# A perceiver layer with routed experts: the entries' product moved into an up product, and a sorted copy of the rows

## The chip, the cores and the metric

The kernel runs on one core of one Trainium2 chip. The metric is the device time of one execution in microseconds (us). Before the change three runs gave 350.67, 354.34 and 351.03 us, median 351.03.

## The reference

One layer over 512 tokens (4 batches of 128 rows, 512 features) and a context of 4 x 2048 rows of 384 features: cross attention, causal self attention, then a feed forward part with one shared expert and 16 routed ones, of which each token takes 4. Each part has its layer norm and its residual. Only the last part is touched:

```python
def _L0_ffn_ref(hidden_states, gate_w, bias_e, up_w, down_w, shared_up, shared_down):
    x2 = hidden_states.reshape(-1, D)                 # 512 x 512
    topk_idx, topk_w = _router(x2, gate_w, bias_e)    # 4 of 16 experts for each token
    combine = jnp.zeros((T, N_EXPERTS)).at[rows, topk_idx].add(topk_w)
    def body(acc, inp):
        wu, wd, cw = inp                              # 256 x 512, 512 x 256
        y = relu2(x2 @ wu.T) @ wd.T
        return (acc + cw[:, None] * y, None)
    routed, _ = jax.lax.scan(body, jnp.zeros_like(x2), (up_w, down_w, combine.T))
    shared = relu2(x2 @ shared_up.T) @ shared_down.T  # inner size 1024
    return (routed + shared).reshape(B, S, D)
x = x + _L0_ffn_ref(_layernorm(x), ...)
```

## The kernel before

Everything is one program written out by hand for each engine; engines wait for one another through named semaphores. PE is the matrix engine, DVE the vector engine, ACT the scalar engine, POOL the general engine, SP the one that issues most DMAs.

The two attentions come first. The last part begins near 195 us. The normalised rows of each batch (`xn`) are turned into columns for the shared expert and are also written to DRAM as `x_rows` (512 x 512). The shared expert is cut into 4 blocks of 256 inner columns. `up(e)` is the up product of a block over all tokens (two halves `m`, each over 4 chunks `c` of the features, 3 matmuls of 512 columns per chunk: 24 matmuls), `down(e)` its down product (24 matmuls, 6 for each batch). Blocks 0 and 1 run in halves, so that PE's end of the shared expert is: `up(2)`, `down_half(0)`, `down_half(1)`, `entries()`, `up(3)`, `down(2)`.

Routing runs on DVE beside this. Each of the 2048 entries (token, expert) gets a position (`pos4`, as integers `pos_int`) in a list sorted by expert, in slots of 32 rows of one expert; 4 slots make a group of 128 rows, and there are 20 groups. `entries()` is a product on PE of two 0/1 tables (`in_row`, `in_group`) which turns "position of an entry" into "entry at a position". From it DVE makes `from_row` (which row of `x_rows` a position takes), `to_row` (where its result goes) and `slot_expert`; `idx_ok` 1 and 2 report them.

The routed experts then run over the groups in pairs. For a group g:

- `gather_rows(g)`: POOL issues an indirect DMA that brings 128 rows from `x_rows` into `xs[g % 4]`;
- `group_rows_T(g)`: PE turns the rows with 4 transposes into a bank; `group_rows(g)`: DVE copies the bank to `xsT`;
- `group_up(g)`, on ACT the relu (`group_hidden`), on PE 2 transposes (`group_hidden_T`), on ACT the square, on PE `group_down(g)`, on ACT `group_results`, and on POOL `scatter_rows(g)` to `y_rows`.

Groups 0 to 3 use one slot of each expert (4 experts a group); groups 4 to 19 have whatever expert their slots need, which DVE and ACT copy out of `WX` ahead of use (`copies_up`, `copies_down`, `copy_up`, `copy_down`). PE's order for a pair is: up of both groups, `group_rows_T(g+2)`, `group_hidden_T` of both, `group_rows_T(g+3)`, down of both. `group_rows_T(0)` stands inside `down(2)`, ahead of its last batch, and `group_rows_T(1)` behind it.

`WX` holds the weights of all 16 routed experts, 1 MB each, in places where other tensors lie earlier; SP loads each when its place is free, in an order written out by hand: 0, 1, 2, 4, 10, 11, 3, 6, 12, 8, 5, 9, 14, 7, 13, 15. Expert 7 waits for `idx_ok` 2, expert 13 for `up(3)`, expert 15 for `down(2)`. `group_up(1)` waits for experts 4 to 7 (`wx_in[1]`), `group_up(3)` for 12 to 15. SP's queue is in order, so is POOL's. At the end SP reads `y_rows` back when `group_up` of the last group is done (`hs_up` at 20), DVE adds, SP writes the output.

Of the kernel before, what the change touches and what calls it, by code (L numbers as in the profile page):

```python
# [36 lines left out]
def layer_program(nc, x, ctx_in, ctxT_in, wqT, wkT, wv, wd, wu, woT, experts, bq, bk, bv, gate, bias_e,  # L37
# [41 lines left out]
    with ExitStack() as es:  # L79
# [119 lines left out]
        onorm = at("onorm", [P, TD], uw_at + 4 * 3 * HALF)  # L199
        cqn = at("cqn", [P, 2 * P], uw_at + 4 * (3 * HALF + TD))  # L200
# [75 lines left out]
        slot_expert = at("slot_expert", [P, ND], gate_at, I32)  # L276
        group_row = at("group_row", [P, NG], hrd_at)
# [21 lines left out]
        pos_int, row_int = (small(n, [P, NK], I32) for n in ("pos_int", "row_int"))  # L299
# [18 lines left out]
        x_rows = nc.dram_tensor("x_rows", (T, D), F32, kind="Internal").ap()  # L318
        y_rows = nc.dram_tensor("y_rows", (T * TOP_K + NG * P, D), F32, kind="Internal").ap()
# [31 lines left out]
        y_ok = sem("y_ok")  # L351
        lgT_mm, lgT_ok = sem("lgT_mm"), sem("lgT_ok")
# [10 lines left out]
        u_lo_pool, d3_in = sem("u_lo_pool"), sem("d3_in")  # L363
        zeros_out, token_ok, ylo_ok, end_mm = (sem(n) for n in ("zeros_out", "token_ok", "ylo_ok", "end_mm"))
# [103 lines left out]
        def _(sp):  # L468
# [66 lines left out]
            for e in (0, 1, 2):  # L535
                load_routed(e)
            for e in range(FIRST):
# [5 lines left out]
            sp.wait_ge(wo_mm, NB)  # L543
            load_routed(10)
# [11 lines left out]
            sp.wait_ge(idx_ok, 2)  # L556
            load_routed(7)
# [3 lines left out]
            load_routed(15)  # L561
            sp.wait_ge(zeros_out, 16 * NL)
            sp.dma_start(d3_w[:].rearrange("p m d -> p (m d)"), experts[NSH - 1, :, HALF:2 * HALF]).then_inc(d3_in, 16)

# [13 lines left out]
        def _(pool):  # L578
# [42 lines left out]
            for g in POOL_LO:  # L621
                pool.wait_ge(cThi_ok, TC * g + 1)
                nc.gpsimd.tensor_tensor(cT[:, g % 2, 1, 0, :], ring_T[:, g % RING_T, 0, :], f32(cT[:, g % 2, 0, 0, :]),  # L623
                                        ALU.subtract).then_inc(cTlo_pool, 1)
            def inverse_root_2(b):
# [63 lines left out]

            def gather_rows(s):  # L690
# [31 lines left out]
            for s in range(NXS, NG + NXS - 1):  # L722
                if s < NG:
                    gather_rows(s)
                if 2 * NXS <= s < 2 * NXS + NL:
                    clear_rows(NG - NL + s - 2 * NXS)
                if s - NXS - 3 >= 0:
                    scatter_rows(s - NXS - 3)
            for s in range(NG - 4, NG - NL):
                scatter_rows(s)  # L730
# [338 lines left out]
        def _(dve):  # L1069
# [128 lines left out]
            def weights():  # L1198
# [7 lines left out]
                dve.wait_ge(cnt_ok, 2)  # L1206
# [9 lines left out]
            def positions():  # L1216
# [4 lines left out]
                dve.wait_ge(numbers, 2)  # L1221
# [16 lines left out]
                link(V_.tensor_copy(pos_int[:], pos4[:]))  # L1238
# [333 lines left out]
            def tokens_of(g):  # L1572

                i = g - (NG - NL)
                dve.wait_ge(xsT_mm, NG - NXS + i + 1)
# [53 lines left out]
        def _(pe):  # L1629
# [86 lines left out]
            def up(e, between=None):  # L1716
# [3 lines left out]
                for m in range(IC):  # L1720
                    for c in range(DC):
# [3 lines left out]
                        if between is not None and m == 0 and c == 1:  # L1725
# [338 lines left out]
            up(2, counts)  # L2064
# [3 lines left out]
            entries()  # L2068
            pe.wait_ge(relu_ok, FIRST + 2)
            up(3)  # L2070
            def group_rows_T(g):
# [7 lines left out]
                for c in range(DC):  # L2079
                    last = nc.tensor.transpose(bank[B_XT[g % 2]][:, c * P:(c + 1) * P], xs[:, g % NXS, c * P:(c + 1) * P], ident[:])  # L2080
# [159 lines left out]
```

## Time and profile before

| | us |
|---|---|
| median of 3 runs (350.67 to 354.34) | 351.03 |
| time of the profiled execution | 353.81 |
| its span, first to last instruction | 352.1 |
| PE busy | 331.0 |
| DVE busy | 239.0 |
| ACT busy | 191.0 |
| POOL busy | 99.7 |

Times in the trace count from the start of the span. "Busy" of PE is modelled, since matmuls overlap, so places are compared by the start times of instructions. The window view gives for a stretch the busy time of each engine with its instruction count, then PEclk (the TensorE clock that was granted, 1.0 is 2.4 GHz, 0.5 is 1.2 GHz), the busy share of the 16 DMA engines and what they moved in GB/s. In a timeline row stand the start, the duration (of all, where it ends with a count), the engine, the line, the operation and its tiles, and in brackets how long the engine was idle before it and who released it.

### The profile page before, as it was taken

The page shows a single profiled execution, that of the slowest core. Times are in us where ns is not written, and L with a number is a line of the kernel's source. Part 1 is how long each engine was busy: PE and PEld are TensorE (multiplying, and loading weights), DVE is VectorE, ACT ScalarE, POOL GpSimd, SP SyncE. Part 2 cuts the span into 40 slices and gives each one's busy share as a digit, 9 for nine tenths or more (in the row PEclk, how much of TensorE's full clock was granted, in tenths as well). Part 3 has the DMA queues.
Part 4 walks back from the last instruction along what each step waited for, and adds up shares of the span by engine and source line. Part 5 has one row for each costly group of instructions (what it writes and reads, how often), then busy time and mean ns, then how long its engine had stood idle before and what let it go on. Part 6 is the DMA issues. An engine that isn't in the chain of part 4 may idle for free.

```text
span 352.1 us, 6990 instructions
## 1 busy us (share of the span) xinstructions
PE 331.0 (94%) x2522; PEld 232.4 (66%) x2522; DVE 239.0 (68%) x480; ACT 191.0 (54%) x432; POOL 99.7 (28%) x114
## 2 busy tenths in 40 slices
PE   6999989999999998997899899989999999999995
PEld 4988756677777756766788779778544544444453
DVE  2875889655489547749976558970546777778586
ACT  2356765525576476466779533302246777777510
POOL 3600400000001311226583420023436755532000
PEclk9899999999999999999999999969999999999999
DMA  6984499975322228017041472898735543321483
GB/s 227 394 345 173 189 371 412 415 256 206 149 95 90 91 90 313 17 65 324 2 152 61 149 270 99 337 400 320 246 101 178 186 178 134 127 98 61 154 325 119
DMA packets 17185, 69.70 MB, mean 198 GB/s; under 512 B 2816, under 2 KB 3328, under 8 KB 14592
## 3 DMA queue, kind: packets, MB, share of 16 engines
q1 hardware_dynamic: 12768, 56.93, 42.9%
q0 software_dynamic: 3520, 11.54, 9.5%
q10 hardware_dynamic: 864, 0.79, 0.7%
q8 instruction: 21, 0.34, 0.4%
q14 instruction: 12, 0.10, 0.1%
HBM read 61.91 MB, written 7.34 MB: 197 GB/s over the span
## 4 chain that ended last, share of the span: by engine, by line
PE 74%; DVE 14%; ACT 6%; issue 3%; DMA 2%; DVEq 0%; POOL 0%; ACTq 0%
PE bank L2111 10%; PE bank L2143 10%; PE bank L1634 9%; PE bank L1636 8%; PE bank L1962 8%; PE bank L1635 8%; PE bank L2080 3%; DVE res L1611 2%; PE bank L1846 2%; DMA raw<-in_wkT 2%; PE bank L1906 2%; PE bank L1803 2%; DVE cT L1321 1%; PE bank L1793 1%; PE bank L2122 1%
## 5 line engine op out<-in xcount | busy, mean ns | idle before, releaser
L1962 PE MATMUL bank<-ring,wT 128*128 128x384 f32 x128 | 44.0, 487 | 0.7 <-ACT wT L905 0.7
L693 POOL DMA_INDIRECT xs<-x_rows,from_row x20 | 23.1, 1154 | 53.8 <-DVE to_row L1275 28.5
L2111 PE MATMUL bank<-WX,xsT 128*32 128x256 f32 (+1 forms) x256 | 36.4, 380 | 0.0
L2143 PE MATMUL bank<-WX,hsT 128*32 128x512 f32 (+1 forms) x128 | 36.2, 595 | 0.0
L1321 DVE TENSOR_TENSOR cT<-ring_T,cT 128x512 fp32r<-128x512 f32 x45 | 30.0, 709 | 6.5 <-ACT cT L757 6.5
L1962 PEld LDWEIGHTS bank<-ring,wT 128*128 128x128 f32 x128 | 23.6, 190 | 14.2 <-ACT wT L905 0.9
L1558 DVE COPY copy<-WX 128x1024 f32 x32 | 20.9, 696 | 13.9 <-PE bank L2143 5.9
L2111 PEld LDWEIGHTS bank<-WX,xsT 128*32 128x32 f32 x256 | 17.1, 110 | 18.8 <-issue 8.4
L757 ACT CAST cT<-ring_T 128x512 fp32r<-128x512 f32 x48 | 27.0, 619 | 4.6 <-PE bank L1636 4.4
L2111 PE MATMUL bank<-copy,xsT 128*32 128x256 f32 x384 | 29.3, 380 | 0.0
L2143 PE MATMUL bank<-copy,hsT 128*32 128x512 f32 x192 | 29.1, 595 | 0.0
L605 POOL TENSOR_TENSOR rstd<-var,mhalf 128x1 f32<-128x1 f32 x12 | 7.5, 625 | 70.8 <-DVE var L1095 70.7
L1565 DVE COPY copy<-WX 128x1024 f32 x32 | 21.2, 703 | 6.1 <-PE bank L2111 4.0
L700 POOL DMA_INDIRECT y_rows<-ys,to_row x16 | 19.0, 1188 | 11.5 <-ACT ys L1015 9.1
L2143 PEld LDWEIGHTS bank<-WX,hsT 128*32 128x32 f32 x128 | 8.2, 109 | 20.2 <-issue 19.9
L1534 DVE COPY xsT<-bank 128x512 f32<-128x512 f32 x20 | 13.1, 685 | 12.5 <-PE bank L2080 12.5
L1041 ACT COPY copy<-WX 128x1024 f32 x16 | 16.8, 1048 | 8.5 <-PE bank L2143 7.2
L1634 PE MATMUL bank<-cT,qk_h 128*128 128x512 f32 x48 | 20.0, 417 | 0.2 <-POOL cT L623 0.2
L1636 PE MATMUL bank<-cT,qk_l 128*128 128x512 f32 x48 | 18.9, 394 | 0.0
L1634 PE MATMUL bank<-xT_l,u_w 128*128 128x256 f32 (+2 forms) x56 | 18.8, 335 | 0.0
L1635 PE MATMUL bank<-cT,qk_h 128*128 128x512 f32 x48 | 18.7, 390 | 0.0
L1636 PE MATMUL bank<-xT_h,u_w 128*128 128x256 f32 (+2 forms) x56 | 18.2, 325 | 0.0
(302 smaller groups left out, 872.5 us busy)
## 6 DMA issues: line engine op xcount, KB each, us to landing
WX<-in_experts SPq DMA_DIRECT2D x16, 1024.0 KB, 6.9
ring_T<-in_ctxT SPq DMA_DIRECT2D x16, 768.0 KB, 7.3
ring<-in_ctx SPq DMA_DIRECT2D x16, 768.0 KB, 4.9
WX<-y_rows SPq DMA_DIRECT2D x4, 1024.0 KB, 9.2
raw<-in_experts SPq DMA_DIRECT2D x3, 1024.0 KB, 4.9
raw<-in_wqT SPq DMA_DIRECT2D x4, 256.0 KB, 5.9
res<-in_x SPq DMA_DIRECT2D x4, 256.0 KB, 7.9
raw<-in_woT SPq DMA_DIRECT2D x1, 1024.0 KB, 5.1
```

The source lines that it names most:

```text
L693: nc.gpsimd.indirect_dma_start(out=xs[:, s % NXS, :], out_offset=None, in_=x_rows, in_offset=bass.IndirectOffsetOnAxis(ap=from_row[:, s:s ...
L700: nc.gpsimd.indirect_dma_start(out=y_rows, out_offset=bass.IndirectOffsetOnAxis(ap=to_row[:, s:s + 1], axis=0), in_=ys[:, s % NYS, :], in_ ...
L757: copy(cT[:, g % 2, 0, t, :], ring_T[:, g % RING_T, t, :]).then_inc(cThi_ok, 1)
L1321: V_.tensor_tensor(cT[:, g % 2, 1, t, :], ring_T[:, g % RING_T, t, :], f32(cT[:, g % 2, 0, t, :]), ALU.subtract).then_inc(cTlo_ok, 1)
L1558: V_.tensor_copy(copies[n % NC][:], WX[:, bass.ds(middle[g][q - 1] * (2 * HALF), HALF)]).then_inc(up_copied, 1)
L1565: V_.tensor_copy(copies[n % NC][:], WX[:, bass.ds(values[q - 1] * (2 * HALF) + HALF, HALF)]).then_inc(down_copied, 1)
L1634: mm(dst, a[0], b[1], start=start, stop=False)
L1635: mm(dst, a[0], b[0], start=False, stop=False)
L1636: return mm(dst, a[1], b[0], start=False, stop=stop)
L1962: last = mm(bank[B_O][:, 0:TD], wT[:, g % 2, k * P:(k + 1) * P], ring[:, g % RING, k, :], start=(c == 0 and k == 0), stop=(c == NCH - 1 an ...
L2111: last = mm(bank[B_H[g % 2]][q * SLOT:(q + 1) * SLOT, 0:IC * P], xsT[:, g % 2, c * P + q * SLOT:c * P + (q + 1) * SLOT], w, start=c == 0, ...
L2143: last = mm(bank[B_Y[g % 2]][q * SLOT:(q + 1) * SLOT, :], hsT[:, g % 2, m * P + q * SLOT:m * P + (q + 1) * SLOT], w, start=m == 0, stop=m ...
```

## The change

Three things. `entries()` is no longer between `down_half(1)` and `up(3)`; `up(3, entries, 2)` runs it behind 9 of its 24 matmuls. Groups 8 to 19 (`GQ` is 8) are no longer gathered and no longer turned on PE: POOL scatters each batch's rows 4 times by `pos_int` into `x_sorted` in DRAM, which SP has filled with zeros before (6 DMAs of 512 KB during the attention), SP loads a pair of groups with 4 DMAs, and DVE's transpose of 32 x 32 blocks writes `xsT` at once. And the up weights of the routed experts, and with them the columns of `xsT`, have another order of features, made on the host. For batches 0 and 1, whose `xn` is gone, SP reads the rows back from `x_rows` into `held`, which lies in expert 7's place, so expert 7's load waits for their 8 scatters too. The core of the diff:

```diff
+                if 0 <= (i := g - 2 * RING_T - 1) < FILLS:
+                    sp.wait_ge(numbers, 2)
+                    rows = slice((GQ + 2 * i) * P, (GQ + 2 * i + 2) * P)
+                    sp.dma_start(x_sorted[rows, :].rearrange("(p n) (h d) -> p (n h) d", p=P, d=BLANK),
+                                 blank[:].unsqueeze(1).to_broadcast([P, 4, BLANK])).then_inc(x_in[NB - 1], 16)
...
             sp.wait_ge(wo_mm, NB)
+
+            for b in range(2):
+                sp.wait_ge(rows_out[b], 16)
+                sp.dma_start(held[:, b, :], x_rows[tok(b), :]).then_inc(x_in[b], 16)
             load_routed(10)
...
             sp.wait_ge(idx_ok, 2)
+            sp.wait_ge(sorted_out[0], 16 * 2 * TOP_K)
             load_routed(7)
...
+            def load_pair(s):
+
+                if s < GQ + NXS:
+                    sp.wait_ge(xsT_mm, s - NXS + 2)
+                else:
+                    sp.wait_ge(xsT_ok, s - NXS + 2)
+                src = x_sorted[s * P:(s + 2) * P, :].rearrange("(n r) (g d) -> g r n d", r=SLOT, g=NQ)
+                for g in range(NQ):
+                    dst = xs[g * SLOT:(g + 1) * SLOT, s % NXS:s % NXS + 2, :].rearrange("r s (q d) -> r (s q) d", q=NQ)
+                    sp.dma_start(dst, src[g]).then_inc(pair_in[s // 2 % 2], 16)
+
+            for h in range(2):
+                sp.wait_ge(sorted_out[h], 16 * 2 * TOP_K)
+            load_pair(GQ)
+            load_pair(GQ + 2)
...
+            def sort_rows(b, rows):
+
+                for k in range(TOP_K):
+                    n = k * NB + b
+                    nc.gpsimd.indirect_dma_start(
+                        out=x_sorted, out_offset=bass.IndirectOffsetOnAxis(ap=pos_int[:, n:n + 1], axis=0),
+                        in_=rows, in_offset=None,
+                    ).then_inc(sorted_out[b // 2], 16)
+
...
+            pool.wait_ge(cnt_ok, 2)
+            pool.wait_ge(x_in[NB - 1], 16 + 16 * FILLS)
+            for b in range(2):
+                pool.wait_ge(x_in[b], 16 * 2)
+                sort_rows(b, held[:, b, :])
...
-            for s in range(NXS):
+            for s in range(GS):
                 gather_rows(s)
-
+            for b in range(2, NB):
+                sort_rows(b, xn[:, norm_no["last", b] % 2, :])
+                for s in range(GS + 2 * (b - 2), GS + 2 * (b - 1)):
+                    gather_rows(s)
+
+            pool.wait_ge(sorted_out[1], 16 * 2 * TOP_K)
...
             def group_rows(g):
-                dve.wait_ge(xsT_mm, g + 1)
                 if g >= 2:
                     dve.wait_ge(hs_up, g - 1)
-                V_.tensor_copy(xsT[:, g % 2, :], bank[B_XT[g % 2]][:]).then_inc(xsT_ok, 1)
+                if g < GQ:
...
+                else:
+
+                    dve.wait_ge(pair_in[g // 2 % 2], 16 * NQ * ((g - GQ) // NXS + 1))
+                    V_.transpose(xsT[:, g % 2, :], xs[:, g % NXS, :].rearrange("p (q k j) -> p q j k", q=NQ, j=DC)).then_inc(xsT_ok, 1)
...
-            entries()
             pe.wait_ge(relu_ok, FIRST + 2)
-            up(3)
+            up(3, entries, 2)
...
-                if g + 2 < NG:
+                if g + 2 < GQ:
                     group_rows_T(g + 2)
-                else:
+                elif g + 2 == NG:
                     last_shared(0)
```

What stands in the engines' programs, at three places. First PE, where the product of the entries (L2060 before, L2120 now) stands; `u_w_75` and `u_w_77` are the up weights of the fourth block, `d_w_77` the down weights of the second. Before:

```order
L1634 MATMUL bank<-d_w_77,gh 128x512
L1635 MATMUL bank<-d_w_77,gh 128x512
L1636 MATMUL bank<-d_w_77,gl 128x512
L2060 MATMUL bank<-in_group,in_row 128x60 [waits relu_ok,ent_ok]
L2060 MATMUL bank<-in_group,in_row 128x60 x15
L1634 MATMUL bank<-xT_l,u_w_75 128x512 [waits u_lo_pool,u_lo,relu_ok]
L1635 MATMUL bank<-xT_h,u_w_75 128x512
```

Now, where 6 more matmuls of the same up product stand ahead of these rows:

```order
L1694 MATMUL bank<-xT_l,u_w_77 128x512
L1695 MATMUL bank<-xT_h,u_w_77 128x512
L1696 MATMUL bank<-xT_h,u_w_77 128x512
L2120 MATMUL bank<-in_group,in_row 128x60 [waits relu_ok,ent_ok]
L2120 MATMUL bank<-in_group,in_row 128x60 x15
L1694 MATMUL bank<-xT_l,u_w_77 128x512
```

The product with its wait for `ent_ok` has moved behind 9 matmuls that wait for nothing of it. Second POOL, from its last index table to the first transfers for the groups; `xs` are the gathered rows. Before:

```order
L597 IOTA entry_no 128x16
L693 DMA xs<-x_rows,from_row 128x512 [waits rows_out3,idx_ok,rows_out2,u_lo_pool,rows_out1,rows_out0]
L693 DMA xs<-x_rows,from_row 128x512 x3
L713 MEMSET zeros 128x512
L693 DMA xs<-x_rows,from_row 128x512 [waits xsT_mm,pool_link]
L693 DMA xs<-x_rows,from_row 128x512 [waits xsT_mm] x3
```

Now:

```order
L634 IOTA entry_no 128x16
L734 DMA x_sorted<-held,pos_int 2560x512 [waits x_in0,x_in3,cnt_ok]
L734 DMA x_sorted<-held,pos_int 2560x512 x3
L734 DMA x_sorted<-held,pos_int 2560x512 [waits x_in1]
L734 DMA x_sorted<-held,pos_int 2560x512 x3
L742 DMA xs<-x_rows,from_row 128x512 [waits rows_out3,idx_ok,rows_out2,u_lo_pool,rows_out1,rows_out0]
L742 DMA xs<-x_rows,from_row 128x512 x3
L734 DMA x_sorted<-xn,pos_int 2560x512 x4
L742 DMA xs<-x_rows,from_row 128x512 [waits xsT_mm] x2
L734 DMA x_sorted<-xn,pos_int 2560x512 x4
L742 DMA xs<-x_rows,from_row 128x512 [waits xsT_mm] x2
```

Eight scatters stand ahead of the first gather, and four ahead of the fifth and of the seventh. Third PE between the up and the down products of a pair, here groups 8 and 9. Before:

```order
L2080 MATMUL bank<-ident,xs 128x128 [waits xsT_ok,xs_in2]
L2080 MATMUL bank<-ident,xs 128x128 x3
L2122 MATMUL bank<-ident,hs 128x128 [waits hsT_ok,hs_ok]
L2122 MATMUL bank<-ident,hs 128x128
L2122 MATMUL bank<-ident,hs 128x128 [waits hsT_ok,hs_ok]
L2122 MATMUL bank<-ident,hs 128x128
L2080 MATMUL bank<-ident,xs 128x128 [waits xsT_ok,xs_in3]
L2080 MATMUL bank<-ident,xs 128x128 x3
```

Now:

```order
L2182 MATMUL bank<-ident,hs 128x128 [waits hsT_ok,hs_ok]
L2182 MATMUL bank<-ident,hs 128x128
L2182 MATMUL bank<-ident,hs 128x128 [waits hsT_ok,hs_ok]
L2182 MATMUL bank<-ident,hs 128x128
```

The 8 transposes of rows are gone there, in the pairs from groups 6 and 7 to groups 16 and 17 (6 pairs); the pairs 0, 2 and 4 keep theirs.

## Rows read from the trace of the kernel before

**Rows 1.** Page: the chain that ended last, share of the span by engine.

```profile
PE 74%; DVE 14%; ACT 6%; issue 3%; DMA 2%; DVEq 0%; POOL 0%; ACTq 0%
```

**Rows 2.** Timeline of PE from the last `down_half` to the second pair.

```profile
228.03 0.39 PE L1636 MATMUL bank<-d_w,gl 128*128 128x512 f32 x1
230.53 3.22 PE L2060 MATMUL bank<-in_group,in_row 128*128 128x60 f32 x16 [2.10 <-DVE in_group L1251]
233.56 0.77 PE L1634 MATMUL bank<-xT_l,u_w 128*128 128x512 f32 x1
...
237.55 0.52 PE L1634 MATMUL bank<-xT_l,u_w 128*128 128x512 f32 x1
...
241.19 0.39 PE L1634 MATMUL bank<-d_w,gh 128*128 128x512 f32 x1
...
245.38 0.60 PE L2080 MATMUL bank<-ident,xs 128*128 128x128 f32 x4
...
247.74 3.66 PE L2111 MATMUL bank<-WX,xsT 128*32 128x256 f32 x64
```

**Rows 3.** Windows: granted clock behind PE's idle time, and the DMA share.

```profile
228.00:230.00 2.00, 0.42 (x2) 0.00 (x0) 1.97 (x5) 0.00 (x0) 0.00 (x0) 1.00 1.11 414
230.00:232.00 2.00, 1.48 (x9) 1.48 (x9) 1.68 (x4) 0.00 (x0) 0.00 (x0) 0.75 0.90 352
232.00:234.00 2.00, 2.00 (x10) 2.00 (x10) 0.18 (x2) 0.00 (x0) 0.00 (x0) 0.50 1.04 426
...
236.00:238.00 2.00, 2.00 (x7) 1.58 (x6) 1.93 (x3) 0.00 (x0) 1.70 (x2) 0.54 0.77 324
```

**Rows 4.** Timeline of DVE: positions, the product's last table, the gathers' rows.

```profile
222.48 0.18 DVE L1238 CAST pos_int<-pos 128x16 int32<-128x16 f32 x1
...
229.99 0.48 DVE L1251 TENSOR_TENSOR in_group<-r_eq,cw_l 128x320 fp32r<-128x320 f32 x1
...
234.62 0.17 DVE L1275 SCALAR_TENSOR_TENSOR to_row<-s_ent,s_free 128x20 int32<-128x20 f32 x1
...
237.95 0.20 DVE L1260 TENSOR_SCALAR slot_expert<-s_exp 128x64 int32<-128x64 f32 x1
```

**Rows 5.** Timeline of POOL: the first two gathers.

```profile
235.74 1.85 POOL L693 DMA_INDIRECT xs<-x_rows,from_row  x1 [28.50 <-DVE to_row L1275]
237.89 0.96 POOL L693 DMA_INDIRECT xs<-x_rows,from_row  x1 [0.30 <-issue]
```

**Rows 6.** DMA from 226 to 237: queue, packets, MB, share of 16 engines.

```profile
q1 hardware_dynamic: 598, 4.37, 100.3%
```

**Rows 7.** DMA issued at 238 to 239: size, us to landing.

```profile
WX<-in_experts SPq DMA_DIRECT2D x1, 1024.0 KB, 7.6
xs<-x_rows,from_row POOLq DMA_INDIRECT x1, 6.8
```

**Rows 8.** Windows: one scatter's DMA time alone; the attention's DMA share.

```profile
100.00:200.00 100.00, 92.42 (x704) 72.24 (x704) 71.61 (x151) 67.03 (x211) 36.22 (x37) 1.00 0.35 127
317.00:321.00 4.00, 3.79 (x67) 2.11 (x60) 3.44 (x7) 3.34 (x5) 2.47 (x2) 1.00 0.19 73
```

**Rows 9.** Timeline, all engines, between the up and down products of a pair.

```profile
294.62 0.63 PE L2080 MATMUL bank<-ident,xs 128*128 128x128 f32 x4
294.66 0.38 ACT L1002 ACTIVATE hs<-bank 128x256 f32<-128x256 f32 x1 [0.41 <-PE bank L2111]
...
295.08 0.60 PE L2122 MATMUL bank<-ident,hs 128*128 128x128 f32 x4
...
295.50 0.66 ACT L1008 ACTIVATE hsT<-bank 128x256 f32<-128x256 f32 x2 [0.46 <-PE bank L2122]
...
296.05 0.62 PE L2143 MATMUL bank<-WX,hsT 128*32 x1
...
296.06 1.28 DVE L1534 COPY xsT<-bank 128x512 f32<-128x512 f32 x2
...
298.15 1.30 DVE L1558 COPY copy<-WX 128x1024 f32 x2 [0.81 <-PE bank L2143]
```

**Rows 10.** Waits of SP: us in total, times, longest; the results' read-back.

```profile
SPq L570 <- PE bank L2111: 7.1, 1, 7.1
```

More of the change, by code:

```diff
@@ L199, in layer_program @@
         onorm = at("onorm", [P, TD], uw_at + 4 * 3 * HALF)
+        GQ = 2 * GS
+        FILLS, BLANK = (NG - GQ) // 2, 2 * P
+        blank = at("blank", [P, BLANK], uw_at + 4 * (3 * D + 2 * P))
+        held = at("held", [P, 2, D], qk_at + 8192)
         cqn = at("cqn", [P, 2 * P], uw_at + 4 * (3 * HALF + TD))
@@ L276, in layer_program @@
         slot_expert = at("slot_expert", [P, ND], gate_at, I32)
+        pos_int = at("pos_int", [P, NK], gate_at + 4 * ND + 128, I32)
         group_row = at("group_row", [P, NG], hrd_at)
@@ L298, in layer_program @@
         cw_h, cw_l = (at(n, [P, NK], gate_at + 4 * ND + 64 * i, F32R) for i, n in enumerate(("cw_h", "cw_l")))
-        pos_int, row_int = (small(n, [P, NK], I32) for n in ("pos_int", "row_int"))
+        row_int = small("row_int", [P, NK], I32)
         r_c = at("r_c", [P, NB * NE * (NE + 1)], raw_at)
@@ L561, in _ @@
             load_routed(15)
+            def load_pair(s):
[11 more added lines that the diff above has]
+            load_pair(GQ + 2)
             sp.wait_ge(zeros_out, 16 * NL)
             sp.dma_start(d3_w[:].rearrange("p m d -> p (m d)"), experts[NSH - 1, :, HALF:2 * HALF]).then_inc(d3_in, 16)
+            for s in range(GQ + NXS, NG, 2):
+                load_pair(s)
             sp.wait_ge(hs_up, NG)
@@ L720, in clear_rows @@
                 ).then_inc(zeros_out, 16)
[L722 to L729, printed above, removed]
+            for s in range(NG - NL):
+                if s < NL:
+                    clear_rows(NG - NL + s)
                 scatter_rows(s)
@@ L1714, in query_constants, with up @@
                 last.then_inc(c_mm, 1)
-            def up(e, between=None):
+            def up(e, between=None, last_c=1):
                 pe.wait_ge(u_lo, 1)
@@ L1724, in up @@
                                         (xT_h[:, c, :], xT_l[:, c, :]), c == 0, c == DC - 1)
-                        if between is not None and m == 0 and c == 1:
+                        if between is not None and m == 0 and c == last_c:
                             between()
@@ L2063, in _ @@
             pe.wait_ge(relu_ok, FIRST + 1)
-            up(2, counts)
+            up(2, counts, 1)
             pe.wait_ge(cnt_ok, 1)
@@ L2079, in group_rows_T @@
                 for c in range(DC):
-                    last = nc.tensor.transpose(bank[B_XT[g % 2]][:, c * P:(c + 1) * P], xs[:, g % NXS, c * P:(c + 1) * P], ident[:])
+                    last = nc.tensor.transpose(bank[B_XT[g % 2]][:, c * P:(c + 1) * P],
+                                               xs[:, g % NXS, :].rearrange("p (k j) -> p j k", j=DC)[:, c, :], ident[:])
                 last.then_inc(xsT_mm, 1)
@@ L2111, in group_up @@
                         last = mm(bank[B_H[g % 2]][q * SLOT:(q + 1) * SLOT, 0:IC * P],
-                                  xsT[:, g % 2, c * P + q * SLOT:c * P + (q + 1) * SLOT], w, start=c == 0, stop=c == DC - 1)
+                                  xsT[:, g % 2, (q * DC + c) * SLOT:(q * DC + c + 1) * SLOT], w, start=c == 0, stop=c == DC - 1)
                 last.then_inc(hs_up, 1)
```

29 lines of the change are left out of this document (20 added, 9 removed).

## The prediction

> **What bounds the kernel now.** I read the chain of the work that ended last first: PE holds 74% of the span [rows 1], so what counts is where PE stands still or does work that need not be there. Then PE's timeline through the last part, for gaps. The reader should see one large gap in it: the last matmul of `down_half` starts at 228.03, the entries' product at 230.53, and the 2.10 us between are a wait for the table `in_group`, which DVE finishes at 229.99 + 0.48 = 230.47 [rows 2, 4]. The windows show what this costs beyond the gap: the granted clock is 1.0 (2.4 GHz) while PE stands, and falls to 0.5 (1.2 GHz) from about 231 to almost 238 [rows 3]. In that stretch the 9 first matmuls of `up(3)` take 237.55 - 233.56 = 3.99, or 0.44 each; the 15 after it 241.19 - 237.55 = 3.64, or 0.24 each [rows 2]. Third, the DMA queues beside this stretch: from 226 to 237 SP's queue alone keeps the 16 engines 100.3% busy with weights of routed experts [rows 6], and only at 236 to 238 the share falls to 0.77 [rows 3], so the weights asked for by then are through at about 237.5. Fourth, one pair of groups, for who waits for whom between its up and down products [rows 9].
>
> The sum is made on the profiled execution's own time, 353.81 us (span 352.1); the median of the runs is 351.03, 2.78 lower, and I carry the difference over to it. What PE gains or loses in the middle reaches the end, since the read-back of the results waited 7.1 us for the last up product [rows 10]; under 1% (3.5 us) either way a measurement can't tell from no change.
>
> **The entries' product.** Now `up(3)` goes on at 228.03 + 0.24 = 228.27; 9 matmuls at 0.24 end at 230.45, and the table is ready at 230.47: no wait, no fall of the clock. The product took 233.56 - 230.53 = 3.03 at half clock; by the two pitches 3.03 x 0.24/0.44 = 1.65 at full clock, so until 232.2; 15 more matmuls take 3.64, until 235.85. Before this point was at 241.19: PE is **5.3 us** ahead. The three quarters of `down(2)` that come next (245.38 - 241.19 = 4.19) bring it to `group_rows_T(0)` at 240.0, not 245.38 [rows 2].
>
> **What then is late.** `group_rows_T(0)` needs the first gather. The table of rows (`to_row`) comes 1.2 us behind the product's end (234.79 against 233.56) [rows 2, 4], now at 233.4. POOL may start its 8 scatters at 222.66, when `pos_int` is made [rows 4]. At 1.85 for the first and 0.96 + 0.30 for each after it, as for the gathers [rows 5], it has issued them by 233.4, so the gather is issued at about 235, a little before the 235.74 of now. But what it asks for stands behind the scatters' data in POOL's queue. A scatter's 256 KB cost 0.19 x 4.0 = 0.76 us of all 16 engines where one stands alone [rows 8]. The least would be its bytes at the 398 GB/s of the weights (4.37 MB in 11 us [rows 6]), 0.66; as most I take twice, 1.5, since beside weights a gather landed after 6.8 us [rows 7]. I take 0.76, the nearest operation. As the engines are full until 237.5, 8 x 0.76 = 6.1 puts weights and scatters together at 243.6. A gather's data (0.76) and half a microsecond to land make `group_rows_T(0)` start at about **244.8**: PE stands 4.8 us in the middle of `down(2)`, and 0.6 is left of the 5.3.
>
> Such a wait lowers the clock again, as 2.1 us did [rows 3]. From `group_rows_T(0)` to the up product of group 1 lie 247.74 - 245.38 + 3.66/2 = 4.2 us of work [rows 2]; at the half clock of the earlier stretch (nearly 7 us long, 1.8 times the pitch) they become at most 7.2, a loss of 3.0. The same up product needs expert 7, which SP now loads only when the 8 scatters have landed, near 244, against 238.1 before (`slot_expert` at 237.95 [rows 4]); its 7.6 us to landing [rows 7] give 251.6. Experts 13 and 15 are queued behind it on SP and come before group 3 needs them, a pair later. Before, that up product started at 247.74 + 1.83 = 249.6. Both bounds lie at 251.6 to 252.0, without loss of clock and with weights in time it is 249.0; I take 251.1. So up to here the change **costs 1.5 us** (from -0.6 to +2.4).
>
> How the two queues share the engines no row here shows. By the Trainium skill, page "DMA: Bandwidth & Descriptors", section "Queues, rings and completion order", each engine goes round between the queue rows and changes only at the end of a packet. Were POOL's writes served in turn so, they and the gather would not be last: the sum would be that of rival 1, below, and not +1.5.
>
> **The groups.** In 6 pairs PE loses 8 transposes of rows. That is not 8 transposes' time: now the first four start at 294.62, `group_hidden_T` at 295.08, the square on ACT at 295.50, the down product at 296.05 [rows 9]. Without them `group_hidden_T` starts at 294.62; the square can't start before ACT has done the relu of the second group, 294.66 + 0.38 = 295.04, and needs the two transposes (0.4 behind their start, as now). So it starts near 295.07, and the down product 0.55 later at 295.62: 0.43 a pair, **-2.6 us** in all. The last four were already beside the square. Bounds: 0.2 a pair if PE waits for the second relu, 0.7 if all the time goes (294.62 to 295.08 and once more half of it); -1.2 to -4.2.
>
> DVE's block transpose has no row. A copy of 1024 columns from SBUF takes 0.65 [rows 9], so 512 take 0.33 at least; twice the copy of 512 from a bank, 1.28, is the most I expect. I take 0.65, as the operation that it replaces (1.28 for two). Up to (1.28 + 0.81)/2 = 1.05 it costs nothing, since DVE idles 0.81 behind the two [rows 9]. By the Trainium skill, "Vector Engine (DVE) Microarchitecture Reference", section 3.8, it does one element per cycle and lane; with VectorE's 0.96 GHz this is an estimate of 0.53, and the sum would be the same.
>
> **At nothing.** The 6 fills (3.1 MB, 7.9 us at 398 GB/s if nothing covered them) lie in the attention, where the DMA share is 0.35 [rows 8]. The two reads into `held` delay experts 10 and 11, which only group 2 needs. The other 8 scatters (6.1 us of DMA) come from about 240 on beside gathers 4 to 7, whose groups are one and two pairs away. The pair loads replace 12 gathers; each has a pair's time, and only if it took longer would the rest be PE's. `scatter_rows(0)` waits behind all sorted writes on POOL; ACT waits for it only at group 4's result. The copies with permuted columns and PE's strided reads for groups 0 to 7 have the sizes of before.
>
> Sum: +1.5 - 2.6 = -1.1, so 353.81 becomes 352.7, and **the median 351.03 becomes 349.9 us**.
>
> **Rivals.** 1, faster: the engines serve POOL's writes as they come, and the weights take the delay. The gather is then in time at 240, experts 5, 9 and 14 are through at 243.6, expert 7 needs 2.6 more and lands at 247.2, 2.4 before the 249.6 of now: -2.4 - 2.6 = -5.0, **346.0** (343.1 if nothing is late: -5.3 - 2.6). For it: POOL can issue from 222.66 on. Against it: there is no free DMA time from 226 to 237 [rows 6].
> 2, slower: a scatter to random rows of DRAM costs more beside weights. At 1.5 the 8 take 12.0, and with the gather `group_rows_T(0)` comes at 251.5; with 3.0 of low clock this is 6.1 + 3.0 - 2.6 = +6.5, **357.5**. It decides from 1.1 a scatter: 237.5 + 9 x 1.1 + 0.5 = 247.9, so 2.5 + 3.0 late, and with a pair saving at its lower bound +4.3, **355.3**. For it: the 6.8 of rows 7. Against it: the 0.76 of rows 8.
> 3, slower: DVE's transpose takes over four copies' time, 2.7: 5.4 - 2.1 = 3.3 in each of 6 pairs, +20, less 2.6: about **370**.
> 4, the transposes' time isn't freed since ACT's chain keeps its length: +1.5, **352.5**.
>
> **Chances.** The forecast 0.42 and rival 4 0.10 stay within 1%; rival 1 has 0.28, rival 2 0.16, rival 3 0.04. So faster 0.28, same 0.52, slower 0.20. The forecast's own range is -0.6 - 4.2 to +2.4 - 1.2: 346.2 to 352.2. To hold 8 in 10 it reaches to the middle of rival 1 and to the point where rival 2 decides: 345.5 to 355.3.
>
> **What would show it.** Right: the entries' product starts within 0.3 us behind the ninth matmul at clock 1.0; then a gap of some 4 us before the first row transpose, released by the gather's DMA, with clock 0.5 behind it; expert 7 issued some 6 us later than now; the down product 1.0 instead of 1.4 us behind the up product's end in the 6 pairs. Wrong: no gap at `group_rows_T(0)` (rival 1); scatters that land later than 245 (rival 2); DVE's transpose over 1.05 us with PE waiting for `xsT` (rival 3); an unchanged distance from up to down (rival 4).

## The result, and the profile after

The changed kernel takes **354.07 us** (median of 22 runs, 352.94 to 355.3). The kernel before, in 22 runs beside it, takes 351.99 (350.67 to 354.34). The ratio is 1.0045, its 95% interval 1.0027 to 1.0064: by the ratio 1.6 us slower, where 1.1 us faster had been forecast. The two profiled executions tell less than that: 353.81 before and 353.79 after, both with a span of 352.1. So the question has two parts: why the profiled executions come out even, and why the medians don't.

The chain of the work that ended last, of the changed kernel, answers [rows 1]:

```profile
PE 64%; DVE 11%; issue 10%; ACT 6%; DMA 4%; POOL 3%; DVEq 0%; ACTq 0%; POOLq 0%
```

PE has 64% instead of 74%; DMA, POOL and "issue" have 17% instead of 5%. The end hangs less on PE's work than before, and more on transfers and on what issues them.

TensorE's timeline of the changed kernel, from the ninth matmul of `up(3)` to the second pair of groups, answers [rows 2] (start, us, engine, line, operation, count, idle time ahead and what ended it; L2120 is the entries' product, L2139 the row transposes, L2171 the up product, L2203 the down product of a group):

```profile
229.95 0.39 PE L1696 MATMUL bank<-xT_h,u_w 128*128 128x512 f32 x1
230.34 1.97 PE L2120 MATMUL bank<-in_group,in_row 128*128 128x60 f32 x16
232.14 0.48 PE L1694 MATMUL bank<-xT_l,u_w 128*128 128x512 f32 x1
...
235.50 0.39 PE L1696 MATMUL bank<-xT_h,u_w 128*128 128x512 f32 x1
...
244.26 0.75 PE L2139 MATMUL bank<-ident,xs 128*128 128x128 f32 x4 [4.15 <-DMA xs<-x_rows,from_row]
...
247.09 1.05 PE L2139 MATMUL bank<-ident,xs 128*128 128x128 f32 x4
248.07 2.18 PE L2171 MATMUL bank<-WX,xsT 128*32 128x256 f32 x32
251.27 1.93 PE L2171 MATMUL bank<-WX,xsT 128*32 128x256 f32 x32 [1.02 <-issue]
```

The product stands behind the ninth matmul without a wait, and `up(3)` ends at 235.7 instead of 241.19. That lead is gone at 244.26: TensorE stood 4.15 us for the first gathered rows. POOL issues this gather at 235.16 (235.74 in [rows 5]), behind its eight scatters, and it lands 9.1 us later (4.2 before). A second wait, 1.02, lies ahead of the up product of group 1 (251.27, before 247.74 + 1.83 = 249.57). The timeline names no releaser for it, but the DMA view shows one that fits: expert 7, without which this product can't start, is asked for at 243.5 (238.2 before) and takes 7.7 us to land, so it is there at 251.2. The DMA issues of the changed kernel from 243.50 to 243.55:

```profile
WX<-in_experts SPq DMA_DIRECT2D x1, 1024.0 KB, 7.7
```

Where expert 7 was asked for earlier (e5, e6, below) the two groups follow each other without a gap. The read-back of the results waits 6.1 us for the last up product (7.1 in [rows 10]), so the end still hangs on TensorE.

The windows of the changed kernel answer [rows 3] (busy time of PE, PEld, DVE, ACT and POOL with counts, then the granted clock, the DMA share, GB/s):

```profile
244.00:246.00 2.00, 1.74 (x8) 1.50 (x9) 0.69 (x1) 0.00 (x0) 1.61 (x2) 0.80 1.02 404
246.00:248.00 2.00, 2.00 (x8) 1.34 (x6) 0.00 (x0) 0.00 (x0) 0.33 (x1) 0.50 1.06 434
248.00:250.00 2.00, 2.00 (x33) 0.99 (x32) 1.82 (x4) 0.00 (x0) 1.28 (x2) 0.84 1.01 422
```

Behind the 4.15 us the clock is at its lower level (0.50) from 246 to 248 and back at the upper one before 250. The DMA share stays at 1.0 from 226 to 260. What the queues did from 226 to 237 answers [rows 6, 7] (packets, MB, share of 16 engines; below them size and us to landing):

```profile
q1 hardware_dynamic: 444, 3.24, 71.5%
q0 software_dynamic: 405, 1.34, 29.9%
issues: line engine op xcount, KB each, median us to landing
WX<-in_experts SPq DMA_DIRECT2D x3, 1024.0 KB, 11.5
x_sorted<-held,pos_int POOLq DMA_INDIRECT x6, 8.7
xs<-x_rows,from_row POOLq DMA_INDIRECT x2, 8.8
```

POOL's queue (q0) takes 30% of the engines' time, SP's (q1) is left with 71.5% of the 100.3% that it had, and both are late: the three experts asked for from 226 on take 11.5 us to land (the four of before 6.1). From 237 to 260 the total moved rises from 5.78 MB (first row, before) to 9.57 MB (second row, the changed kernel):

```profile
DMA packets 1199, 5.78 MB, mean 251 GB/s; under 512 B 208, under 2 KB 208, under 8 KB 784
```

```profile
DMA packets 2126, 9.57 MB, mean 416 GB/s; under 512 B 370, under 2 KB 370, under 8 KB 1547
```

The loop does gain. Transposes of the hidden rows in the third and in the ninth pair, of before and then of the changed kernel:

```profile
269.32 0.60 PE L2122 MATMUL bank<-ident,hs 128*128 128x128 f32 x4
...
321.15 0.60 PE L2122 MATMUL bank<-ident,hs 128*128 128x128 f32 x4
```

```profile
271.43 0.60 PE L2182 MATMUL bank<-ident,hs 128*128 128x128 f32 x4
...
321.13 0.74 PE L2182 MATMUL bank<-ident,hs 128*128 128x128 f32 x4 [0.20 <-issue]
```

The changed kernel comes to the third pair 2.11 us late and to the ninth on time: the six pairs take 49.70 instead of 51.83, 0.36 less each. From there to the end the two traces agree within 0.03 us.

### The profile page after: what moved, and what is told of

It reads as the page before. It is cut to its first block, busy times and chain, and to the rows that moved or that the text cites. A ratio compares the mean times of both kernels' runs of the same rounds, so it can differ in the third digit from the quotient of the medians.

```text
span 352.1 us, 6922 instructions
## 1 busy us (share of the span) xinstructions
PE 326.7 (93%) x2474; PEld 226.0 (64%) x2474; DVE 244.1 (69%) x480; ACT 192.0 (55%) x432; POOL 104.8 (30%) x119
## 4 chain that ended last, share of the span: by engine, by line
PE 64%; DVE 11%; issue 10%; ACT 6%; DMA 4%; POOL 3%; DVEq 0%; ACTq 0%; POOLq 0%
PE bank L2171 10%; PE bank L2203 10%; PE bank L2022 8%; PE bank L1694 6%; PE bank L1696 6%; PE bank L1695 6%; POOL x_sorted L734 3%; DMA xs<-x_rows,from_row 3%; PE bank L1906 2%; DVE res L1671 2%; PE bank L1966 2%; DMA raw<-in_wkT 2%; PE bank L1863 2%; PE bank L2139 1%; PE bank L2182 1%
## 5 line engine op out<-in xcount | busy, mean ns | idle before, releaser
L2171 PE MATMUL bank<-WX,xsT 128*32 128x256 f32 (+1 forms) x256 | 37.0, 385 | 1.0 <-issue 1.0
L2203 PE MATMUL bank<-WX,hsT 128*32 128x512 f32 (+1 forms) x128 | 36.2, 595 | 1.0 <-ACT hsT L1061 0.8
L2171 PEld LDWEIGHTS bank<-WX,xsT 128*32 128x32 f32 x256 | 17.3, 112 | 20.4 <-issue 10.3
L749 POOL DMA_INDIRECT y_rows<-ys,to_row x16 | 20.3, 1267 | 32.9 <-ACT ys L1068 31.6
L2171 PE MATMUL bank<-copy,xsT 128*32 128x256 f32 x384 | 29.3, 380 | 0.0
L2203 PE MATMUL bank<-copy,hsT 128*32 128x512 f32 x192 | 29.1, 595 | 0.0
L2203 PEld LDWEIGHTS bank<-WX,hsT 128*32 128x32 f32 x128 | 8.2, 109 | 21.3 <-issue 20.8
L1055 ACT ACTIVATE hs<-bank 128x256 f32<-128x256 f32 x20 | 7.7, 386 | 22.3 <-PE bank L2171 21.9
L1694 PE MATMUL bank<-xT_l,u_w 128*128 128x256 f32 (+2 forms) x56 | 17.9, 319 | 0.0
L1695 PE MATMUL bank<-xT_h,u_w 128*128 128x256 f32 (+2 forms) x56 | 17.5, 312 | 0.0
L1696 PE MATMUL bank<-xT_h,u_w 128*128 128x256 f32 (+2 forms) x56 | 17.5, 312 | 0.0
```

The source lines that it names most:

```text
L749: nc.gpsimd.indirect_dma_start(out=y_rows, out_offset=bass.IndirectOffsetOnAxis(ap=to_row[:, s:s + 1], axis=0), in_=ys[:, s % NYS, :], in_ ...
L1694: mm(dst, a[0], b[1], start=start, stop=False)
L1695: mm(dst, a[0], b[0], start=False, stop=False)
L1696: return mm(dst, a[1], b[0], start=False, stop=stop)
L2171: last = mm(bank[B_H[g % 2]][q * SLOT:(q + 1) * SLOT, 0:IC * P], xsT[:, g % 2, (q * DC + c) * SLOT:(q * DC + c + 1) * SLOT], w, start=c == ...
L2203: last = mm(bank[B_Y[g % 2]][q * SLOT:(q + 1) * SLOT, :], hsT[:, g % 2, m * P + q * SLOT:m * P + (q + 1) * SLOT], w, start=m == 0, stop=m ...
```

## The experiments

Two questions are tested: what the medians of before stand on (e1, e9, e13, e14, and e3 on the way), and what holds group 1 and so eats the lead (e2 to e8, e11, e12). e10 prices VectorE's transpose. Ratios are against the kernel before, run on the same chip beside each. The code of an edit is shortened.

**e1, e9: before, unchanged.**

> The kernel before, not changed at all, to see what its executions have in common. Theory A: the profiled execution of before (353.81) is one in which the 2.10 us wait for in_group took TensorE's clock down ([rows 3]: 0.5 of full speed from 231 to 238, an estimated 2.8 us from the durations of [rows 2]); in others the clock stays up. Then the executions fall into two groups, near 351.3 and near 353.8, those of the upper group with a mean granted clock about 0.01 lower (7 us of 352 at half speed). Rival B: the clock falls in every execution and the spread has another source; then the mean clock is the same, 0.983, in short and long executions.

> The kernel before once more, for a profile. Theory A, as for the first repetition: if this execution takes under 352.5, the granted clock stays at 1.0 from 231 to 238 although TensorE waits 2.1 us for in_group, and up of group 0 starts near 245 instead of 247.74; if it takes over 353, the clock falls as in [rows 3]. Rival B: clock and starts as in [rows 2, 3] whatever the time.

e1 is before itself: ratio 1.0013 (0.9979 to 1.0046). Its 12 executions and the 29 beside them lie mostly in two groups: 18 under 352.5 with a median of 351.7 and a mean clock of 0.989, 23 over it with 353.8 and 0.984. The clock differs in the expected direction by half of the expected 0.01, and it doesn't sort every execution: four of the long ones have 0.987 or more, three of the short ones 0.984. e9's execution took 351.89. The windows behind TensorE's wait for `in_group`, of e1's profiled execution (354.49) and of e9's:

```profile
231.00:238.00 7.00, 7.00 (x27) 5.94 (x27) 4.84 (x16) 0.00 (x0) 2.40 (x2) 0.55 0.96 398
```

```profile
231.00:238.00 7.00, 7.00 (x28) 5.67 (x28) 4.08 (x14) 1.23 (x2) 3.76 (x3) 0.76 0.97 394
```

The same wait of 2.09 us is followed by 0.55 in the one and by 0.76 in the other; up of group 0 starts at 245.21 in e9 instead of 247.74:

```profile
229.62 1.97 PE L2060 MATMUL bank<-in_group,in_row 128*128 128x60 f32 x16 [2.09 <-DVE in_group L1251]
...
245.21 3.66 PE L2111 MATMUL bank<-WX,xsT 128*32 128x256 f32 x64
```

So the loss differs between executions; "1.0 in every short one" does not hold. Only 1.6 of the 2.5 us come from this stretch: 0.9 lies ahead of 229 in e9 (the product starts at 229.62, not 230.53), and that lead is there by 21 us (the same transposes start at 20.24 in e9 and at 21.14 in before). The granted clock in 40 equal slices of the span (tenths, 9 is 90% or more), of before and then of e9, shows beside the fall in slice 27 an earlier one in slice 2 of before (from 10 to 12 us it is at 0.50), which e9 doesn't have:

```profile
PEclk9899999999999999999999999969999999999999
```

```profile
PEclk9999999999999999999999999989999999999998
```

So the spread of before has more than one source. How much of it the wait is answerable for, the next two experiments show.

**e13, e14: before with TensorE busy in the wait, and with a longer wait.**

```
 # e13, in entries(), ahead of the wait for in_group
+pe.wait_ge(relu_ok, IC * FIRST + 1)
+for _ in range(8):
+    mm(bank[B_POST][:], xT_h[:, 0, 0:P], xT_h[:, 0, :], start=True, stop=True)
 # e14, in rows_of_groups(), ahead of the last in_group
+for _ in range(3):
+    link(V_.tensor_tensor(in_group[:, :, 2 * NG:3 * NG], r_eq[:], ..., ALU.mult))
```

> Before with eight matmuls of 128x512 on resident data (8 x 0.235 = 1.9 us, their result is overwritten) in TensorE's 2.10 us wait for in_group; nothing else is moved, the product starts when it did. Theory A: the executions of before are long where the clock falls behind this wait and short where it doesn't; without the idle time it never falls, so all executions lie with the short ones, 350.5 to 352.5, median 351 to 351.7 (that of before lies between 352 and 353.4), mean clock 0.99 or more. Rival B, the spread has another source: executions above 353 remain as frequent as before (about half).

> Before with three more multiplications of 128x320 (0.48 us each) on VectorE ahead of the last table, so TensorE waits 3.5 us for in_group instead of 2.10. Theory A: the clock falls in every execution; all lie 1.4 above the long ones of before, 354.8 to 355.8, none under 354. Rival B: half of the executions are 1.4 above the short ones, near 353.1.

e13: 350.61 (350.04 to 351.28, 9 runs), ratio 0.993 (0.9903 to 0.9958), with 9 of the 18 runs of before beside it above 353. e14: 355.34 (354.56 to 357.32), ratio 1.008 (1.0049 to 1.011), no run under 354. Both go as theory A has it, though e13's median lies 0.4 under its range and e14's longest run 1.5 over. TensorE in e13:

```profile
228.23 2.02 PE L2059 MATMUL bank<-xT_h 128*128 128x512 f32 x8
230.47 1.97 PE L2062 MATMUL bank<-in_group,in_row 128*128 128x60 f32 x16 [0.22 <-DVE in_group L1251]
...
244.59 3.66 PE L2113 MATMUL bank<-WX,xsT 128*32 128x256 f32 x64
```

The product starts when it did in [rows 2], its 16 matmuls take 1.97 instead of 3.22, and up of group 0 starts at 244.59. Eight useless matmuls bring 2.6 us in the median, and the runs of e13 lie within 1.2 us where those of before beside it spread over 3.7: most of the spread was the clock behind this wait. Between the start of the product and up of group 0 the fall cost 3.1 us in before (247.74 - 230.53 = 17.21 against 244.59 - 230.47 = 14.12 in e13) and still 1.5 in e9 (15.59), one of the short executions. e14's profiled execution, its shortest, has a wait of 3.66 and comes to group 0 at 247.86, only 0.12 later than before, with a mean clock of 0.76 from 231 to 238: a longer wait isn't followed by a longer fall each time, and what e14 shows lies in its ten times.

**e3: the changed kernel with the product in its old place.**

```
+entries()
 pe.wait_ge(relu_ok, FIRST + 2)
-up(3, entries, 2)
+up(3)
```

> The changed kernel with the entries' product back in its old place ahead of up(3). Theory A: group 1 is held by expert 7, which lands near 251.3 whatever TensorE did before, so this takes what the changed kernel takes, 353.5 to 354.5, and moving the product is worth nothing beside the sorted copy. Rival D, the time that the moved product saved is still in the changed kernel's time and something in the loop ate it: then this is slower than the changed kernel by 2.5 to 5, 356.5 to 359.

353.8 (352.84 to 355.99), ratio 1.0045 (1.0016 to 1.0074): what the changed kernel takes. TensorE in e3:

```profile
230.44 1.97 PE L2120 MATMUL bank<-in_group,in_row 128*128 128x60 f32 x16 [2.10 <-DVE in_group L1305]
...
244.65 0.75 PE L2140 MATMUL bank<-ident,xs 128*128 128x128 f32 x4 [2.33 <-DMA xs<-x_rows,from_row]
...
251.34 1.93 PE L2172 MATMUL bank<-WX,xsT 128*32 128x256 f32 x32 [2.20 <-issue]
```

The wait of 2.10 is back, behind it the clock stayed up this time (the product takes 1.97), and group 1's up product starts at 251.34 as in the changed kernel (251.27): expert 7 is asked for at 243.5 here too and takes 7.7 us. Beside the sorted copy the moved product is worth nothing: what comes earlier on TensorE waits longer.

**e2, e8, e11: before with the product moved, alone and with expert 13 later.**

```
 # e2
-entries()
 pe.wait_ge(relu_ok, FIRST + 2)
-up(3)
+up(3, entries, 2)
 # e8 as e2, and on SP (e11: xs_in[1])
+sp.wait_ge(xs_in[3], 16)
 load_routed(13)
```

> Before with the entries' product inside up(3) and nothing else of the change. Theory A: there is no wait, so no fall of the clock in any execution; up(3) ends at 235.9, the first gather is issued near 234.4 and lands before the 240.0 at which TensorE comes to the first row transposes; the loop is as before. Up of group 1 starts at 244.3 instead of 249.6 if expert 7 (issued near 236) has landed, so 348.5 (353.8 - 5.3), one group of executions. Rival C, the gather or expert 7 is late in a full queue as in the changed kernel: up of group 1 at 246 to 249, 350 to 353.

> Before with the entries' product inside up(3), as in the run with that alone, and expert 13's load (needed by group 3 alone) behind the landing of gather 3. There TensorE waited 2.46 us for gather 1 at the second row transposes while experts 7 and 13 were in flight. Theory A (order of the transfers): that wait goes to under 0.5, up of group 0 at 241.5 to 242 instead of 244.17, time 348 to 348.7 against 350.5 without this. Rival: expert 7 itself is then what group 1 waits for, up of group 1 at 244 to 246 as before, 350 to 350.5.

> Before with the entries' product inside up(3), and expert 13's load behind the landing of gather 1 instead of gather 3. Theory A: gather 1 lands as in the run with gather 3 (1.10 us of wait instead of 2.46), expert 13 is issued about 1 us earlier than there, so group 3 waits 0.7 instead of 1.65: 349.5 to 350. Rival H (volume): what the rows gain the expert loses, 350.4 as both other versions.

e2: 350.49, ratio 0.9955 (0.9923 to 0.9986). e8: 350.4, 0.9952 (0.9919 to 0.9985). e11: 350.03 (349.5 to 351.19, 6 runs), 0.9904 (0.9866 to 0.9942). All three beat both kernels; their intervals overlap, so none is shown to be the best of them, and e13's useless matmuls do as well. The changed kernel is e2 with the sorted copy and its order of features: 1.0045 against 0.9955, so these cost 0.9%, their gain in the loop included. In e2 the lead reaches the second row transposes and stops there, as rival C said:

```profile
243.59 0.66 PE L2079 MATMUL bank<-ident,xs 128*128 128x128 f32 x4 [2.46 <-DMA xs<-x_rows,from_row]
244.17 3.66 PE L2110 MATMUL bank<-WX,xsT 128*32 128x256 f32 x64
```

With expert 13 behind gather 3 (e8) this wait is 1.10, and group 3 waits instead, for expert 15, which SP asks for behind 13 (at 245.5, landing 9.8 us later, at 255.3). Theory A's wait under 0.5 did not come, and the expert that is late is not the rival's 7. The wait of group 3 in e8:

```profile
255.44 1.93 PE L2111 MATMUL bank<-WX,xsT 128*32 128x256 f32 x32 [1.65 <-issue]
```

With 13 behind gather 1 (e11) the wait is 1.73 and group 3 hardly waits (0.1). Three of e2's 12 executions took 352.0 to 354.0 at clocks of 0.990 to 0.995; why is open.

**e4, e6, e7: the changed kernel with the transfers in another order.**

```
 # e4, POOL: gathers 0 to 3 ahead of the scatters of blocks 0 and 1
-for b in range(2): sort_rows(b, held[:, b, :])
 for s in range(GS): gather_rows(s)
+for b in range(2): sort_rows(b, held[:, b, :])
 # e6: held in expert 11's place; 7 waits for no scatter, 11 is loaded last
+held = at("held", [P, 2, D], wx_place(11))
 # e7: block 0 as before; block 1 held in 11's place, scattered behind gather 3
+held = [at("held0", [P, D], qk_at + 8192), at("held1", [P, D], wx_place(11))]
```

> The changed kernel with POOL's gathers 0 to 3 ahead of the eight scatters from held (expert 7 still waits for those). Theory A: the first gather lands by 240 and the 4.15 us wait of TensorE at the first row transposes is gone, but the scatters are issued from 239.5 to 249.5, expert 7 is issued near 250 and lands near 257; up of group 1 at 257 instead of 251.3, 358 to 360. Rival E, the rows and not expert 7 hold group 1: up of group 1 at 247 to 249, 350 to 352.

> The changed kernel with held in the place of expert 11, whose load is issued last; expert 7 waits for no scatter. Theory G, the wait of expert 7's load is what holds group 1: gather 0 as before at 244.3, but group 1 follows group 0 without a gap, up of group 1 at 249.9 instead of 251.27, 352.4 to 352.8. Theory H, the transfers are full in that stretch and whatever is issued earlier takes its time from the others: the first row transposes start later by up to 2.5 (1 MB at 0.42 MB a us), up of group 1 at 251 to 252.5, 353.8 to 355.

> The changed kernel with only token block 0 scattered ahead of gathers 0 to 3; blocks 1, 2 and 3 follow behind gathers 3, 5 and 7. Block 1 is held in the place of expert 11, which is loaded last; expert 7 waits for four scatters. By theory A (order of the transfers) the first row transposes start at 240, up of group 1 at 245 to 247 instead of 251.27, the loop keeps its gain of 2.1 over before: 348 to 350. Rival H (volume): expert 11, 13 or 15 is late instead and group 2 or 3 waits: 352 to 355.

All three are slower than the changed kernel: 362.33 (ratio 1.0264, 1.0209 to 1.0318), 359.05 (1.017, 1.0116 to 1.0224) and 360.42 (1.0205, 1.0169 to 1.0241). One row of TensorE each, the wait that took over, in this order:

```profile
257.48 3.64 PE L2171 MATMUL bank<-WX,xsT 128*32 128x256 f32 x32 [13.17 <-issue]
```

```profile
246.78 1.13 PE L2139 MATMUL bank<-ident,xs 128*128 128x128 f32 x4 [5.70 <-DMA xs<-x_rows,from_row]
...
263.66 4.96 PE L2171 MATMUL bank<-WX,xsT 128*32 128x256 f32 x64 [2.90 <-issue]
```

```profile
264.36 5.13 PE L2172 MATMUL bank<-WX,xsT 128*32 128x256 f32 x64 [8.82 <-issue]
```

In e4 the rows are in time (239.94) and group 1 waits 13 us for expert 7, asked for at 251.9 and landing 5.4 us later, at 257.3. In e6 expert 7 is asked for early, at 237.7: the rows come later (a wait of 5.70, not 4.15), and expert 11 is late for group 2 (250.9 + 12.7 = 263.6). In e7 it is group 2 that waits 8.82, for expert 11 (255.4 + 8.8 = 264.2). Theory G and theory A's times for e7 fall; rival H holds in kind, but the losses are larger than it had them. Part of that is the clock: the long waits are followed by the lower level (a mean of 0.50 from 246 to 252 in e6).

**e5, e12: the changed kernel without half of the scatters.**

```
 # e5: no loads into held, no sort_rows(0) and (1), no wait of expert 7
 # e12: no sort_rows(2) and (3), no waits for them
```

> The changed kernel without the loads into held and the eight scatters of token blocks 0 and 1 (their rows of the sorted copy stay zero, so part of the experts' work is done on zeros), and with expert 7 issued at once; the other eight scatters stay. Theory A: those eight scatters and what they hold up (gather 0 behind them, expert 7 behind them) are the whole delay of group 1. The first row transposes start at 240.0 instead of 244.26, up of group 1 at 244 to 246 instead of 251.27, time 348 to 349.5. Rival F, the other eight scatters and the loads of the experts fill the transfers as much: up of group 1 at 249 or later, 352 to 354.

> The changed kernel without the eight scatters of token blocks 2 and 3 (their rows of the sorted copy stay zero, so part of the experts' work is done on zeros); the early eight and the wait of expert 7's load for them stay. Theory H (volume): expert 7 is issued near 243.6 as before but shares the transfers with 2 MB less, lands 2 to 3 us earlier, up of group 1 at 248.5 to 249.5 instead of 251.27, 351.5 to 352.5. Rival J, only the early eight matter: up of group 1 at 251, 353.5 to 354.

Both leave rows of the sorted copy at zero. e5: 348.7, ratio 0.989 (0.9844 to 0.9936), 1.5% or 5.4 us under the changed kernel; up of both first groups runs through from 243.91. e12: 353.58, ratio 1.0004 (0.9975 to 1.0034); its up of group 1 comes 19.5 us behind the product's start instead of 20.9, a gain of 1.4 of the 2 to 3 expected. Expert 7 itself takes 5.2 us to land there, not 7.7, as theory H has it, but then the first rows hold both groups (a wait of 4.08). The early eight scatters, with the loads into `held` and expert 7's wait, are the main price, the late eight a small one.

**e10: one transpose more in each pair.**

```
+if g % 2 == 0: link(V_.transpose(xsT[:, g % 2, :], xs[:, g % NXS, :]...))
```

> The changed kernel with the block transpose of every even group from 8 to 18 done twice on VectorE (1.12 us more for each of six pairs). VectorE is idle for 0.94 to 1.39 of the 8.2 to 8.3 us of a pair in the changed kernel, all of it where it waits for TensorE. If the transposes lie beside other work, as the prediction put them, this adds 0 to 0.2 a pair, 354 to 355.3. Rival I, VectorE has become what a pair's length hangs on: each us of it shows, 6 x 1.12 = 6.7 more, 360 to 361.

355.44 (354.38 to 356.04), ratio 1.0061 (1.0036 to 1.0086) against the changed kernel's 1.0045: 0.6 by the ratios and 1.4 by the medians, of 6.7 us added. Most of the added time lies beside other work.

## Why the prediction was wrong

**What failed first: carrying the difference of one profiled execution over to the median.** The prediction saw that the median lay 2.78 us under the profiled execution, and took the change's -1.1 from both. But the profiled execution of before is one of the long ones, 1.82 over the median of its 22 runs, and that of the changed kernel is not (0.28 under). What makes most of the difference is how far the clock falls in the stretch of [rows 3]: 3.1 us in the profiled execution, 1.5 in e9's; removing the fall is worth less in the shorter executions, and e13 shows 350.0 to 351.3 for all once TensorE is kept busy. The changed kernel, on the other hand, is held at group 1 by transfers, and comes there at 251.3 with the wait for `in_group` or without it (e3). For an execution of before as e13's, in which up of group 1 starts at 244.59 + 1.83 = 246.42, the bill is 251.27 - 246.42 = +4.85 up to there, +0.41 in the first pairs, -2.13 in the loop: 350.61 + 3.1 = 353.7, the changed kernel's time. For the profiled one, with 249.57, it is +1.70 + 0.41 - 2.13 = 0.0. The median of before lies between. Of the 2.7 us between the forecast of -1.1 and the +1.6 by the ratio, this step is 1.6; the other 1.1 are the terms of the sum.

**The terms of the sum**, against the profiled execution:

| step | predicted | measured |
|---|---|---|
| `up(3)` ends, no wait | 235.85 | 235.7 |
| first row transposes start | 244.8 | 244.26 |
| up of group 1 | 251.1 (+1.5) | 251.27 (+1.70) |
| groups 1 to 5 | 0 | +0.41 |
| six pairs of the loop | -2.6 | -2.13 |
| sum | -1.1 | 0.0 |

- The entries' product: right, to 0.15 us.
- What then is late: right, place, releaser and size. 8 scatters at 0.76 us beside weights put the rows at 244.8, and they came at 244.26. The clock behind the wait stood low for 3 to 4 us, not 7; expert 7, landing at 251.2, set the start of group 1, as the second of the two bounds had it (251.6).
- At nothing: wrong by 0.41. The row transposes of groups 2 to 7 read `xs` with a stride now. In a pair two sets of four take 0.72 to 0.75 and 0.64 us instead of 0.63 to 0.66 and 0.60, which makes some 0.35 of it up to the third pair; the waits ahead of them are no longer than before (0.17 and 0.22 against 0.23 and 0.22). That the other eight scatters hide is nearly right (e12).
- The loop: right in kind, mis-sized in this execution: 0.36 a pair, not 0.43. From the first transposes behind the up product to the down product it takes 288.90 - 287.92 = 0.98 us, against 296.05 - 294.62 = 1.43 in [rows 9]: 0.45 less, about the 0.43. But the transposes now wait for ACT's relu inside, as rival 4 had it, and TensorE stands about 0.1 us ahead of them. How the gain and the 0.41 ahead of it split differs between executions: e3, with the same loop, has 49.31 for the six pairs and loses 0.56 ahead of them. Both together, from the transposes of hidden rows in the first pair to those in the ninth, the changed kernel takes 67.41, e3 67.37 and before 69.33. Timeline of the changed kernel, in one pair:

```profile
287.89 0.39 ACT L1055 ACTIVATE hs<-bank 128x256 f32<-128x256 f32 x1 [0.41 <-PE bank L2171]
...
287.92 0.84 PE L2182 MATMUL bank<-ident,hs 128*128 128x128 f32 x4
...
288.37 0.82 ACT L1061 ACTIVATE hsT<-bank 128x256 f32<-128x256 f32 x2
...
288.90 0.61 PE L2203 MATMUL bank<-WX,hsT 128*32 x1
...
289.25 2.24 DVE L1594 STREAM_TRANSPOSE xsT<-xs 128x512 f32<-128x512 f32 x2
```

- VectorE's transpose takes 1.12 us, not 0.65, and more than the 1.05 given as its cover. It costs next to nothing all the same: VectorE was idle elsewhere in the pair too, none of TensorE's waits in the trace is put down to `xsT`, and one more transpose in each pair brings 0.1 to 0.2 us a pair (e10).

**The rivals.** Rival 1 fell, though its rule did not. (Its own sum has a slip: 243.6 + 2.6 put expert 7 at 246.2, not 247.2.) By the Trainium skill, page "DMA: Bandwidth & Descriptors", section "Queues, rings and completion order", an engine goes round the queue rows and changes at the end of a packet; the trace agrees, with 405 packets of POOL's queue beside 444 of SP's from 226 to 237. But POOL's are smaller (1.34 MB against 3.24 MB), so its queue gets under a third of the bytes, and the gather stands at the end of that same queue. Rival 2's scatter of 1.1 us or more did not come: the eight and the gather were through at 244. Rival 3 fell (1.12 us, hidden). Rival 4 took 0.07 a pair.

What the prediction lacked is a case in which the first half of the change is worth nothing because the second half sets the time. The rows for it were there: group 1 was bounded by expert 7 at 251.6, whenever TensorE came. With a bound that does not hang on TensorE's arrival, what the arrival gained should have counted as zero, and an execution of before that arrives earlier as a loss.

## What to carry to other kernels

When a change puts a bound by transfers where a bound by work was, reckon from the new bound and not from the time saved: here it came at 251.27 and 251.34 in two executions in which TensorE waited 4.15 and 2.33 us for the first rows, while up of group 0 in before came at 245.21 to 247.78. Look in several executions for what the profiled one alone may have (here a fall of the clock), before its difference is carried to a median; a few useless matmuls in a wait tell what the clock's part of it is. And where the DMA engines are full from end to end, as here, another order of the transfers may only choose who waits: e4, e6 and e7 each moved the wait, and leaving transfers out (e5) took it away.

## What was not expected of the hardware

- The same idle time of TensorE, 2.09 to 2.10 us, was followed by a mean granted clock from 231 to 238 of 0.55 in e1, 0.76 in e9 and, with the product at full pace, by no fall in e3. The Trainium skill, page "TensorE: Matmul & The Clock Gate", section "Part 1: The HAM clock gate", says of a kernel's start that the count of matmuls at the lower level varies between runs of one kernel; the traces show the like behind a wait in the middle of one.
- VectorE's block transpose of 128x512 (four bytes an element, read with a stride of four elements) takes 1.12 us in a pair of two, twice the 0.53 that the prediction estimated from the Trainium skill, "Vector Engine (DVE) Microarchitecture Reference", section 3.8; the measurement decides.
- A set of four row transposes on TensorE whose rows are read with a stride of four elements takes 0.04 to 0.09 us longer (0.64 and 0.72 in the changed kernel, 0.60 and 0.63 in before, at a granted clock of 1.0). The stride is all that the instructions differ in; no run changes it alone.
